# Performer attention and FFN on eight cores: pieced first K chunks, shifted first norms, earlier W2 loads, last block summed by columns

## What is computed

```
Q, K, V = x Wq^T / 8, x Wk^T / 8, x Wv^T              # 16 heads of 64
phi(y)  = exp(y.proj - max(y.proj)) * exp(-|y|^2 / 2) + 1e-6      # 256 features a head
KV      = sum_t phi(K)_t V_t,  Ksum = sum_t phi(K)_t
attn    = phi(Q) KV / (phi(Q) Ksum + 1e-6)
x1      = layernorm(x + attn Wo^T + bo)
out     = layernorm(x1 + relu(x1 W1 + b1) W2 + b2)
```

## Time and profile before

| | |
|---|---|
| runs | 1597.09, 1597.8, 1600.97 us; median 1597.8 |
| profiled execution | 1598.6 us, its slowest core's span 1597.1 us |
| spans of the eight cores | 1584.7 to 1597.1 us |
| PE busy | 1553.8 us (97%) |
| DVE, ACT, POOL busy | 639.1, 735.8, 563.2 us |
| PE's wait for W2 (`w`) near 1150 us, core 7 and core 4 | 4.0 and 2.4 us |
| second Wk piece: ACT's cast of it starts at | 15.37 us |
| chain that ended last | PE 89%, DVE 4%, DMA 3%, issue 2%, ACT 2% |

### The profile page before, as it was taken

One profiled execution on the slowest core, in us unless ns is written; L12 is line 12 of the kernel. 1 busy time (PEld: TensorE's weight loads), 2 busy tenths in 40 slices (PEclk: granted clock), 3 DMA queues, 4 the chain that ended last, 5 costly groups with the idle time before them and its releaser, 6 DMA issues.

```text
span 1597.1 us, 28373 instructions; the slowest of 8 cores (1584.7 to 1597.1 us)
## 1 busy us (share of the span) xinstructions
PE 1553.8 (97%) x9848; PEld 718.4 (45%) x9848; DVE 639.1 (40%) x1374; ACT 735.8 (46%) x1668; POOL 563.2 (35%) x480
## 2 busy tenths in 40 slices
PE   8899999998989999999999999999899999999997
PEld 3355555554434444444444444444344444444443
DVE  4577777776754444444444444200011111111111
ACT  3577777776755556555555665444211111011111
POOL 4366666762444434443443433100121111111110
PEclk9999999998989999999999999999999999999999
DMA  9566678329785956758576577638964414433110
GB/s 187 131 119 109 107 107 131 70 48 243 177 141 140 195 143 137 183 143 181 132 175 154 131 168 155 152 102 128 164 249 165 148 57 165 165 101 124 60 54 40
DMA packets 255068, 218.70 MB, mean 137 GB/s; under 512 B 200912, under 2 KB 201424, under 8 KB 251472
## 3 DMA queue, kind: packets, MB, share of 16 engines
q1 hardware_dynamic: 244384, 184.34, 43.7%
q0 software_dynamic: 10544, 32.54, 14.1%
HBM read 137.45 MB, written 68.16 MB: 129 GB/s over the span
## 4 chain that ended last, share of the span: by engine, by line
PE 89%; DVE 4%; DMA 3%; issue 2%; ACT 2%; POOL 0%; SPq 0%; DVEq 0%; ACTq 0%; POOLq 0%
PE bk L73 53%; PE ps L73 36%; DVE maxa L81 2%; DMA w<-W 1%; ACT eq L74 1%; DMA wk0f<-WkT 1%; DVE r L79 1%; DMA mgt<-mrg 0%; DVE qk L76 0%; DVE mrg L77 0%; DVE bia L79 0%; DVE rden L82 0%; ACT e L74 0%; SPq L62 0%; ACT qk L75 0%
## 5 line engine op out<-in xcount | busy, mean ns | idle before, releaser
L81 DVE TENSOR_REDUCE maxa<-ps 128x4 f32<-128x1024 f32 x256 | 312.4, 1220 | 155.5 <-PE ps L73 155.3
L74 ACT ACTIVATE eq<-ps,bia 128x256 bf16<-128x256 f32 x512 | 200.7, 476 | 219.1 <-DVE bia L79 176.2
L73 PE MATMUL ps<-rt,w 128*128 128x512 bf16 x1032 | 241.1, 379 | 0.0
L74 ACT ACTIVATE e<-ps,bia 128x256 bf16<-128x256 f32 x512 | 201.2, 478 | 81.7 <-DVE bia L79 78.9
L73 PE MATMUL bk<-rt,w 128*128 128x512 bf16 x1016 | 237.6, 379 | 0.0
L73 PE MATMUL bk<-w,ht 128*128 128x512 bf16 x1024 | 225.1, 381 | 4.0 <-DMA w<-W 4.0
L73 PE MATMUL ps<-w,ht 128*128 128x512 bf16 x1024 | 223.6, 379 | 0.0
L74 ACT ACTIVATE jnk<-out,nmu 128x1024 bf16<-128x1024 f32 x32 | 36.7, 1148 | 389.1 <-DVE nmu L78 389.1
L78 POOL TENSOR_SCALAR eq<-eq 128x1024 bf16<-128x1024 bf16 x96 | 100.2, 1043 | 319.1 <-ACT eq L74 317.3
L77 POOL TENSOR_TENSOR out<-rn,b2b 128x1024 f32<-128x1024 bf16 x32 | 68.2, 2135 | 354.9 <-DMA out<-out 334.8
L78 POOL TENSOR_SCALAR e<-e 128x1024 bf16<-128x1024 bf16 x128 | 133.5, 1043 | 103.3 <-ACT e L74 98.7
(11 more groups left out here) (88 smaller groups left out, 1416.6 us busy)
## 6 DMA issues: line engine op xcount, KB each, us to landing
h_d<-hts SPq DMA_DIRECT2D x112, 256.0 KB, 2.7
ht<-h_d SPq DMA_DIRECT2D x14, 2048.0 KB, 14.8
r<-x SPq DMA_DIRECT2D x32, 512.0 KB, 5.7
out<-out SPq DMA_DIRECT2D x32, 512.0 KB, 2.9
x_d<-xb SPq DMA_DIRECT2D x8, 1024.0 KB, 6.4
xb<-x_d SPq DMA_DIRECT2D x8, 1024.0 KB, 7.5
r1n_d<-r1n SPq DMA_DIRECT2D x32, 256.0 KB, 4.3
w<-W POOLq DMA_DIRECT2D x4, 2048.0 KB, 19.1
```

What stands on the lines that cost most here:

```text
L73: "matmul": lambda g, *a, **k: g.matmul(*a, **k),
L74: "activation": lambda g, *a, **k: g.activation(*a, **k),
L81: "reduce_max": lambda g, *a, **k: g.reduce_max(*a, **k),
```

## The change

Four things. (1) SP issues x and Wk pieces in turns (x0, wk0, x1, wk1, x2, x3); POOL's queue starts on `wk0f[0]` (second in order) in place of `x0f[1]` (second in order before); chunks 0 and 1 are summed together, two slices `d` at a time as they arrive, into banks 5 and 4, with 26, 6, 12 and 8 matmuls on zeros ahead of the four pieces (52 in place of 40). (2) `first_norms(g + 1)` moves into the `between` of `features(3, g)`, `first_norms(0)` stands behind chunk 2, and `next_norms` keeps 2 pending in place of 1. (3) Quarters 0, 1, 2 of W2 are issued at s = 61, 65, 66, the last one when 6 of the last 42 `up` products are done. (4) For m = 31 the columns are summed in three parts (512, 256, 256), each added and put through `bn_stats` while PE works on the next; mean and variance come from `bn_aggr`; the last normalization and the store go in two halves.

```diff
+    x0f, wk0f = [], []
+    for k in range(4):
+        x0f.append(load(sp, f"s_x0_{k}", ...))
+        if k < 2:
+            wk0f.append(load(sp, f"s_wk0_{k}", ...))
...
-    pool.wait(x0f[1])
+    pool.wait(wk0f[0])
...
-    for k in range(40):
-        pe.do("matmul", BK[6], WARM[:, 0:128], WARM[:, :], start=True, stop=True)
+    for k, n in enumerate((26, 6, 12, 8)):
+        warm_up(n)
+        pe.wait(x0_cast[k], wk0_cast[k // 2])
+        for c in range(2):
+            for d in (2 * k, 2 * k + 1):
+                first = pe.do("matmul", BK[5 - c], WKQ[0][:, 0, d, c * 128:(c + 1) * 128],
+                              XB[0][:, d, :], start=(d == 0), stop=(d == 7), mark=(d == 7))
+            if k == 3:
+                use_chunk(0, c, 5 - c, first, act if c == 0 else dve, pool)
...
-    def next_norms(keep=1):
+    def next_norms(keep=2):
...
-    for c in range(3):
-        proj_chunk(0, c, 4 + (c + 1) % 2, dve if c % 2 else act)
+    proj_chunk(0, 2, 5, act)
+    first_norms(0)
     for g in range(4):
         for su in range(4):
-            if su == 0:
-                first_norms(g)
-            features(su, g, su % 2, between=next_norms)
+            def between():
+                next_norms()
+                if su == 3 and g < 3:
+                    first_norms(g + 1)
+            features(su, g, su % 2, between)
             next_sum()
...
+        if s in (61, 65, 66):
+            pool.wait(xb_done[15] if s == 61 else num_done[63, 3])
+            load_w2(max(0, s - 64))
...
-    pool.wait(xb_done[15], num_done[63, 3], mgt_done[63])
     while up_n[0] < 256:
-        if up_n[0] - n0 in (4, 15, 26, 37):
-            pool.wait(up_tok[0])
-            load_w2((up_n[0] - n0 - 4) // 11)
+        if up_n[0] - n0 == 6:
+            pool.wait(mgt_done[63], up_tok[0])
+            load_w2(3)
...
+    def last_down(m):
+        toks = []
+        for b, c0, n in LAST_PARTS:
+            pe.wait(*free[b])
+            for ic in range(32):
+                tok = pe.do("matmul", BK[b][:, 0:n], HT..., W2[ic // 8][:, ic % 8, c0:c0 + n], ...)
+            toks.append(tok)
+        return toks
+
+    def last_ln2(m, toks):
+        o, b = OUT[m % 3], blk_of(m)
+        dve.wait(rn_done[m])
+        for j, (bk, c0, n) in enumerate(LAST_PARTS):
+            dve.wait(toks[j])
+            t = dve.do("tensor_tensor", out=o[:, c0:c0 + n], in0=BK[bk][:, 0:n],
+                       in1=o[:, c0:c0 + n], op=ALU.add, mark=True)
+            dve.wait(t)
+            t = dve.do("bn_stats", out=BNS[:, 6 * j:6 * j + 6], in_=o[:, c0:c0 + n], mark=True)
+        dve.wait(t)
+        t = dve.do("bn_aggr", out=MV[:, :], in_=BNS[:, :], mark=True)
+        act ... Ln, Exp on 128x1
+        for c0 in (0, 512):
+            t = dve.do("tensor_scalar", out=o[:, c0:c0 + 512], ...)
+            out_done[m] = sp.dma(s_out[m % 3], out_h[...c0:c0 + 512], o[:, c0:c0 + 512])
+    LAST_PARTS = [(0, 0, 512), (1, 512, 256), (2, 768, 256)]
```

More of the change, by code:

```diff
@@ L80 @@
     "transpose": lambda g, *a, **k: g.transpose(*a, **k),
+    "bn_stats": lambda g, *a, **k: g.bn_stats(*a, **k),
+    "bn_aggr": lambda g, *a, **k: g.bn_aggr(*a, **k),
     "reduce_max": lambda g, *a, **k: g.reduce_max(*a, **k),
@@ L181, in build_program @@
     RSTD = [small(f"rstd{i}", [128, 1], F32, 4) for i in range(2)]
+    BNS = small("bns", [128, 18], F32, 72)
+    MV = small("mv", [128, 2], F32, 8)
     assert SBUF_BASE + sm[0] <= 229368, sm[0]
@@ L250, in keep_x @@
         x_kept[ti] = load(sp, f"s_xd{ti}", rows(x_d[ti]), by4(XB[XBUF[ti]][:, :, :]))
[L253 to L257, removed]
+    x0f, wk0f = [], []
+    for k in range(4):
+        x0f.append(load(sp, f"s_x0_{k}", flat(X0F[:, 2 * k:2 * k + 2, :]),
+                        xT_h[0, :, k * 1024:(k + 1) * 1024]))
+        if k < 2:
+            wk0f.append(load(sp, f"s_wk0_{k}", flat(WK0F[:, 4 * k:4 * k + 4, :]),
+                             Wk_h[0, :, k * 1024:(k + 1) * 1024]))
     warm_ready = dve.do("memset", WARM[:, :], 0.0, mark=True)
@@ L262, in build_program @@
     act.do("activation", out=LNV[0][:, :], in_=EPSC[:, :], func=AF.Exp)
+    x0_cast, wk0_cast = [], []
     for k in range(4):
         dve.wait(x0f[k])
-        xb_ready[0] = dve.do("tensor_copy", XB[0][:, 2 * k:2 * k + 2, :],
-                             X0F[:, 2 * k:2 * k + 2, :], mark=True)
+        x0_cast.append(dve.do("tensor_copy", XB[0][:, 2 * k:2 * k + 2, :],
+                              X0F[:, 2 * k:2 * k + 2, :], mark=True))
+    xb_ready[0] = x0_cast[3]
     for k in range(2):
         act.wait(wk0f[k])
-        wk0 = act.do("copy", out=WKQ[0][:, 0, 4 * k:4 * k + 4, :],
-                     in_=WK0F[:, 4 * k:4 * k + 4, :], mark=True)
-    pool.wait(x0f[1])
+        wk0_cast.append(act.do("copy", out=WKQ[0][:, 0, 4 * k:4 * k + 4, :],
+                               in_=WK0F[:, 4 * k:4 * k + 4, :], mark=True))
+    wk0 = wk0_cast[1]
+    pool.wait(wk0f[0])
     ind_ready = load(pool, "s_ind", IND[:, :], ind_h[:, :])
@@ L345, in proj_chunk, with use_chunk @@
             xb_done[ti] = tok
-        ev, sq = ev or act, sq or pool
+        use_chunk(ti, c, b, tok, ev or act, sq or pool)
+        return tok
+    def use_chunk(ti, c, b, tok, ev, sq):
         ev.wait(tok)
@@ L355, in proj_chunk @@
                                   in1=QK[ti % 2][:, c, :], op=ALU.mult, mark=True)
-        return tok
     def norms(ti, c):
@@ L755, in build_program, with warm_up @@
     pe.wait(warm_ready)
-    for k in range(40):
-        pe.do("matmul", BK[6], WARM[:, 0:128], WARM[:, :], start=True, stop=True)
+    def warm_up(n):
+        for _ in range(n):
+            pe.do("matmul", BK[6], WARM[:, 0:128], WARM[:, :], start=True, stop=True)
+    for k, n in enumerate((26, 6, 12, 8)):
[7 more added lines that the diff above has]
+                use_chunk(0, c, 5 - c, first, act if c == 0 else dve, pool)
     def first_norms(g):
@@ L1011, in ln2 @@
         out_done[m] = sp.dma(s_out[m % 3], out_h[b * 128:(b + 1) * 128, :], o[:, :])
+    def last_down(m):
[3 more added lines that the diff above has]
+            for ic in range(32):
+                tok = pe.do("matmul", BK[b][:, 0:n],
+                            HT[(m // 4) % 3][ic // 16][:, ic % 16, m % 4 * 128:(m % 4 + 1) * 128],
+                            W2[ic // 8][:, ic % 8, c0:c0 + n],
+                            start=(ic == 0), stop=(ic == 31), mark=(ic == 31))
+            toks.append(tok)
[11 more added lines that the diff above has]
+        t = dve.do("bn_aggr", out=MV[:, :], in_=BNS[:, :], mark=True)
+        act.wait(t)
+        t = act.do("activation", out=LNV[0][:, :], in_=MV[:, 1:2], func=AF.Ln,
+                   scale=1.0, bias=EPSC[:, :], mark=True)
+        act.wait(t)
+        t = act.do("activation", out=RSTD[0][:, :], in_=LNV[0][:, :], func=AF.Exp,
+                   scale=-0.5, mark=True)
+        dve.wait(t)
+        for c0 in (0, 512):
+            t = dve.do("tensor_scalar", out=o[:, c0:c0 + 512], in0=o[:, c0:c0 + 512],
+                       scalar1=MV[:, 0:1], scalar2=RSTD[0][:, :], op0=ALU.subtract, op1=ALU.mult,
+                       mark=True)
+            sp.wait(t)
+            out_done[m] = sp.dma(s_out[m % 3], out_h[b * 128:(b + 1) * 128, c0:c0 + 512],
+                                 o[:, c0:c0 + 512])
+    LAST_PARTS = [(0, 0, 512), (1, 512, 256), (2, 768, 256)]
     sp.wait(up_done)
@@ L1021, in build_program @@
         resid(m)
+        if m == NSUB - 1:
+            last_ln2(m, last_down(m))
+            break
         ev = ffn_down(m)
```

## The result

The changed kernel takes 1602.96 us (median of 9 runs), the kernel before 1598.82 (9 runs on the same chip): ratio 1.0029, 95% interval 1.0019 to 1.0040. It is 0.3% **slower**. The forecast was 1584.3 with a range up to 1589.5, so it was wrong, by direction as well. Three of the nine runs of either kernel fell into a slow state (1630 us and more; on the changed kernel some cores had a lower granted clock in them): they count in the medians, not in the ratio. The changed kernel's profiled execution took 1602.0 us, its slowest core's span is 1600.5.

What follows compares the result with a forecast made beforehand. PE, 97% busy, was taken as the bound, leaving gaps, slow clock and both ends; core 7: 1.1 + 5.9 + 5.8 + 1.9 = 14.7 off 1598.6, giving 1583.9, core 4 1584.5; forecast 1584.3, range 1580.5 to 1589.5.

Steps and rivals of the forecast that it cites:

- the price of part 3: Early W2 loads beside the last attention steps' transposing loads: costed at 0, bounds -0.5 and +3 us.
- Rival (c): Early W2 loads from s = 61 slow transposing loads to near 14 us, six PE stops: 1603 us; chance 0.02.
- Part 2 (norms): First stage, norms one step later: 5.7 us of waits and 1.75 of clock won, 1.5 given back: 5.9 us.
- Part 3's gain: Second product near 1155 us: wait for W2's last quarter and fall of clock go, 5.8 us on core 7.
- Part 4: Last block in column parts: shorter chain and store after the last matmul, 1.9 us less, bounds 1.0 and 2.6.
- Part 1: Pieced start: features 3.2 us earlier, but x tile 1 leaves 1.1 us on core 7, 0 on core 4.
- my sum of the start: PE's list for the first two chunks: 1.9 + 68 matmuls at 0.216 + 1.5 + about 1 of waiting = 19.1.
- a sign of being wrong: The prediction called itself wrong if, among other signs, the first 80 us give under 4 us.
- Rival (a): Start: PE's new wait of about 2 us for x tile 1 costs the clock, 1.75 us: 1586.1; chance 0.25.
- Rival (b): First stage bound by DVE at 2.5 us a step: 1587.2 us on core 7, core 4 near 1588; chance 0.18.

Runs made afterwards that it cites:

- e8: As e7, but quarter 0 of W2 goes out in eight pieces of 256 KB, one at each g of s = 61 and 62: 1588.4 us, 0.9937 to the kernel before.
- e2: The kernel before with the early W2 loads alone: 1606.4 us, ratio 1.0057 to the kernel before.
- e7: e3 with only quarter 0 of W2 moved to s = 61, in one piece, quarters 1 to 3 at products 1, 11, 21: 1596.1 us, 0.9981.
- e5: The kernel before with the norms one step later alone: 1593.7 us, ratio 0.9963 to the kernel before.
- e3: As e1, but W2 loads at the 1st, 11th, 21st and 31st of the last 42 products: 1588.8 us, 0.9938 to the kernel before.
- e1: The changed kernel with W2 loaded as before, behind the attention: 1593.6 us, ratio 0.9971 to the kernel before.
- e6: The kernel before with the pieced start alone: 1599.3 us, ratio 1.0004 to the kernel before.

## Why the prediction was wrong, point by point

**The step that failed is the price of part 3**: "The load may take three times as long before PE feels it. I cost it at 0; bounds -0.5 (DMA free for other loads at 1141) and +3." The first sentence was right: at 10.5 us (e8) PE feels nothing, at 17.3 to 19.5 it waits 1.2 to 5.0; PE had 12.6 and 13.4 us to spare at the two long waits. The second didn't follow from it. Nothing in the prediction worked out how long a transposing load would take beside 2 MB of W2; it took five times as long, not up to three. The price was 14.4 us on core 7, and the early loads alone cost 9 us net of their gain (e2). Even the bound of +3 did not enter the forecast's own range, which has 1.5 + 1 us on either side. Two views of the kernel before could have shown the danger. One is the busy time in one of these steps, with a DMA share of already

```profile
939.00:960.00 21.00, 20.75 (x132) 9.29 (x131) 10.63 (x26) 12.74 (x29) 7.96 (x7) 1.00 0.65 154
```

(and 0.86 in the step before), and a quarter of W2 takes some 18 us to land. The other is the first `eta` load of that trace, issued at 359.95 us beside other transfers of SP's queue, with a DMA share of 1.14 from 360 to 365 us. It held the queue for 7 us and took 10.6 to land:

```profile
359.95 6.98 SPq L68 DMA_TRANSPOSE eta<-eq  x1
```
```profile
eta<-eq SPq DMA_TRANSPOSE x1, 10.6
```

Yet the sum of DMA time is a warning, not the mechanism: e8 moves the same bytes in the same two steps without loss. What counts, as e7 against e8 shows, is the burst in one piece. The Trainium skill ("DMA: Bandwidth & Descriptors", Queues, rings and completion order) says that each DMA engine serves its queues in turn and drains a whole packet of one before it goes on to the next. The small transfers of SP's queue would then get one turn for each packet of W2. 3.8 us becoming 18 does not speak against it, but no run here shows single turns, so why the loads are slow stays open.

**Rival (c) was the right one, at a chance of 0.02.** It named the place (s = 61 on), the loads (`mgt`, `eta`), the point from which it decides (near 14 us) and 1603 us, and I gave it up because "the same loads took at most twice that with DMA full". That was a wrong reading: the 10.6 us above are three times 3.5, and that was DMA filled by SP's own transfers, without a burst from POOL's queue. That it met the measured time is in part luck: three loads came late, not six, but two of the three waits were longer than its 3.2 us (4.8 and 5.0) and followed by half clock, and the gains that it set against them were 14 us where 11 came. I had left out the clock, which makes such a wait dearer (3.9 us behind 11.0 of waiting), and the transposing loads beside quarter 1. POOL's queue, which I did check, was no problem.

**Point by point.** Part 2 (norms) 5.9 forecast, 5.9 measured (e5): the waits for squares and `maxa` went as forecast, but that the two figures agree is luck, with a new wait of 2.0 us in the one and an interval of 4.0 to 7.8. Part 3's gain 5.8 forecast, 5.5 measured on core 7, 5.3 by the smaller shift (e3 against e1). Part 4, 1.9 forecast, 2.0 by the chain; `bn_stats` of 256 columns took 0.43 us where 0.42 was taken, and the columns set PE's pace. Part 1 was forecast to give core 7 1.1 us and won nothing (e6). Features start at 24.2 us in place of 21.9, since the two chunks ended at 20.3 and not at 19.1 (the first Wk piece came late) and chunk 2 then stood 1.91 us for its own quarter of Wk, a transfer that my sum of the start didn't have. It ends at x tile 1, as forecast, but that chunk starts at 38.17, where it started at 37.49 before: the transfer that releases POOL's queue landed later on this core, x tile 1 was issued at 14.99 in place of 14.06 and landed at 37.9 in place of 36.3. The sums of V start at 60.55, 3.3 us earlier than the 63.83 of before (the prediction has 70 for it): under the 4 us that the prediction named as a sign of being wrong. The row of chunk 2 is in the timeline of PE:

```profile
22.19 1.89 PE L73 MATMUL bk<-xb,wk 128*128 128x512 bf16 x8 [1.91 <-DMA wk<-WkT]
```

Rival (a) came true in part: core 7 waited 1.85 us for x tile 1, and its clock was low behind it (0.93 from 25 to 50 us), as on cores 2 and 6 with 2.8 and 2.7 us; core 1 waited 2.3 us and kept its clock. It may be why start and norms together gave no more than the norms; no run separates it. Rival (b) came near on core 7: the six steps from 44.27 to 60.55 us took 2.7 us each (its condition was 2.5, the forecast's 2.3), with waits for a bias in between,

```profile
52.46 0.24 PE L73 MATMUL bk<-ind_sb,sq 128*128 128x2 bf16 x4 [1.16 <-DVE bia L79]
```

and start and norms gave 3.6 us there, where it had 3.7. Against it stand e5's 5.9 us for the norms alone and leads of 4.8 to 6.8 us on five cores. How much of the missing gain is DVE's pace and how much x tile 1 with its clock stays open.

The measured parts add up: +0.0004 (start), -0.0037 (norms), -0.0009 (last block), +0.0057 (W2 early) make +0.0015, measured is +0.0029, within the intervals of the four.

## What to carry to other kernels

Before a long transfer is moved to beside short ones that somebody waits for, ask what the short ones will take while it runs, and read that from a row with such a burst; where none exists, the loss must be a serious rival, and a slack of twice the normal landing is not enough. If the data must come early, cut the transfer into pieces with gaps and look for loads that fall between two of them, or move it only as far as its own wait asks: here 6 products (10 us) sooner gave all that 31 sooner could give. And price a new wait of PE with the lower clock behind it, here a third as much again.

## What the runs showed that I had not expected

- 2 MB of W2 from POOL's queue made transposing loads on SP's queue take 17.3 to 19.5 us in place of 3.5 to 3.8, and a plain store of 256 KB there 18.0 in place of 3.8; the issue of one load held SP's queue for 13.45 us; in pieces of 256 KB the load took 10.5 and the issue 5.43.
- Quarter 0 of W2 took 27.8 us in these steps, quarter 1, which had transposing loads beside it too, 17.7, and quarter 2 17.6.
- After idling of 1.9 us for x tile 1 the clock fell on one core, after 2.3 it did not on another, nor after 3.0 on core 0 of e1; the length of the idle time alone doesn't tell.
- `bn_stats` over 256 f32 columns took 0.43 us, over 512 0.69: the mean and variance of a row cost DVE no more than an add of the same width.
